# Late sums and table steps after the first trio's critical step, and Q's last stores between the loads of Q's tiles

## The reference

```
Q, K, V = x @ Wq, x @ Wk, x @ Wv              # 8 heads of 64
score   = exp(clip((K[src] * Q[dst]).sum(-1) / 8, -5, 5))   # per edge and head
wV, Z   = segment_sum(V[src] * score, dst), segment_sum(score, dst)
h       = x + wV / (Z + 1e-6)
out     = layernorm(x + batchnorm(h) * gamma + beta)        # batchnorm over nodes
```

## Time and profile before

| | us |
|---|---|
| median of 3 runs | 1886.88 |
| profiled execution, device time | 1886.89 |
| its span | 1885.0 |
| TensorE, VectorE, ScalarE, GpSimd busy | 1843.9, 1726.0, 1427.3, 1235.8 |

### The profile page before, as it was taken

How to read it: one execution, slowest core, us unless ns; L and a number is a source line. 1 busy time by engine, 2 the same in 40 slices (tenths; PEclk the granted TensorE clock), 3 DMA queues, 4 the chain that set the end, 5 groups by cost and what they waited for, 6 DMA issues and landing times.

```text
span 1885.0 us, 41041 instructions
## 1 busy us (share of the span) xinstructions
PE 1843.9 (98%) x7561; PEld 1290.4 (68%) x7672; DVE 1726.0 (92%) x2608; ACT 1427.3 (76%) x4699; POOL 1235.8 (66%) x1424
## 2 busy tenths in 40 slices
PE   8999999998999999999999999999999999999897
PEld 4444444446788887888888888888888888877333
DVE  8877776667999999999999999999999999999898
ACT  1112221126999999999999999999999999998867
POOL 1221112116888888888888888888888888875677
PEclk9999999998999999999999999999999999999999
DMA  5676667658999999999999999999999999999317
GB/s 207 221 252 223 223 222 247 235 195 316 365 364 358 354 356 357 372 357 360 349 365 373 348 354 358 368 357 357 345 368 362 361 360 353 369 360 370 118 34 290
DMA packets 191291, 589.09 MB, mean 313 GB/s; under 512 B 29104, under 2 KB 30864, under 8 KB 191248
## 3 DMA queue, kind: packets, MB, share of 16 engines
q0 software_dynamic: 135904, 465.14, 67.1%
q1 hardware_dynamic: 51888, 121.69, 17.8%
q10 hardware_dynamic: 3456, 1.78, 0.4%
HBM read 535.27 MB, written 78.91 MB: 326 GB/s over the span
## 4 chain that ended last, share of the span: by engine, by line
PE 57%; DVE 23%; issue 7%; DMA 7%; ACT 3%; POOL 2%; ACTq 1%; POOLq 0%; SPq 0%; DVEq 0%
PE places L390 21%; PE acc L1110 21%; PE q_ps L1094 12%; DVE kv L968 9%; DVE raw L979 7%; DMA kv<-kv_d,idx 5%; POOL kv L924 2%; DVE stats L1463 1%; ACT kv L1019 1%; DVE agg L1447 1%; PE mm_ps L1120 1%; DVE agg L1456 1%; DVE raw L972 1%; DMA q_tile<-xb_d 1%; DVE kv L886 1%
## 5 line engine op out<-in xcount | busy, mean ns | idle before, releaser
L924 POOL DMA_INDIRECT kv<-kv_d,idx x880 | 892.8, 1014 | 242.0 <-issue 202.9
L1019 ACT ACTIVATE kv<-kv 128x64 f32<-128x64 f32 x3520 | 889.1, 335 | 14.3
L1110 PE MATMUL acc<-kv,mm_rest 128*128 128x260 f32 x2640 | 634.6, 383 | 3.5 <-POOL kv L886 2.2
L1110 PEld LDWEIGHTS acc<-kv,mm_rest 128*128 128x128 f32 x2640 | 489.9, 189 | 105.1 <-issue 27.7
L968 DVE TENSOR_TENSOR kv<-q_ps,kv 128x1024 f32<-128x1024 f32 x440 | 536.5, 1219 | 16.5 <-DMA kv<-kv_d,idx 10.7
L979 DVE TENSOR_REDUCE raw<-kv 128x16 f32<-128x1024 f32 x440 | 533.1, 1212 | 0.0
L1094 PE MATMUL q_ps<-q_tile,mm_rest 128*128 x1320 | 422.1, 441 | 5.1 <-DVE kv L968 4.9
L390 PE MATMUL places<-w_sb,s_sb 128*128 128x512 f32 x704 | 305.9, 593 | 3.4 <-issue 3.1
L1094 PEld LDWEIGHTS q_ps<-q_tile,mm_rest 128*128 128x128 f32 x1320 | 247.6, 189 | 53.7 <-DVE kv L968 10.4
L886 DVE TENSOR_TENSOR kv<-kv 128x384 f32<-128x384 f32 (+1 forms) x440 | 272.3, 619 | 0.0
L390 PEld LDWEIGHTS places<-w_sb,s_sb 128*128 128x128 f32 x704 | 133.1, 190 | 172.9 <-issue 165.3
(11 more groups left out here) (202 smaller groups left out, 1482.8 us busy)
## 6 DMA issues: line engine op xcount, KB each, us to landing
kv_d<-kv SPq DMA_DIRECT2D x98, 256.0 KB, 2.2
q_tile<-q_d SPq DMA_DIRECT2D x49, 512.0 KB
kv<-kv_d,idx POOLq DMA_INDIRECT x880, 6.4
xb<-in_x POOLq DMA_DIRECT2D x49, 256.0 KB, 4.2
xb_d<-xb POOLq DMA_DIRECT2D x49, 256.0 KB, 6.5
out_rows<-agg SPq DMA_DIRECT2D x49, 256.0 KB, 2.1
x_sb<-in_xT SPq DMA_DIRECT2D x16, 768.0 KB, 6.5
q_d<-q_c SPq DMA_DIRECT2D x16, 512.0 KB, 2.6
```

The lines of the kernel that those rows point to most:

```text
L924: pool.indirect_dma_start(kv[:, s, u, 0:2 * DIM], None, kv_d, bass.IndirectOffsetOnAxis(idx[:, s, u:u + 1], 0), bounds_check=N_NODES - 1, ...
L1019: return act.activation(v, v, ACT.Copy, scale=kv[:, s, u, 2 * DIM + h:2 * DIM + h + 1])
L1110: last = pe.matmul(acc[:, bass.ds(par, 1), DIM - (1 - n) * HALF:DIM + n * HALF], m, kv[:, sc, u, DIM + n * HALF:DIM + (n + 1) * HALF], sta ...
```

## The change

The last x sums of trio 0 (X3, X8, X7) and T8 move from ahead of the loop to behind k_out(0) of trio 0. All numbered table steps come two slots later (`tables(3g - 2)`, `(3g - 1)`, `(3g)` for `(3g)`, `(3g + 1)`, `(3g + 2)`), ScalarE's `sign` with them, and `ends` comes just ahead of step 0. The four last Q stores leave project; in attend SyncE does two loads, a store, two loads, a store, and so on for four stores, then the loads up to tile 39, a wait for all stores, and the rest.

```diff
@@ project, sync
-                if g == TRIOS - 1:
-                    sp.wait_ge(soft["s_g0"], 32)
-                store_q(c, split_of(g, 2), q_c, s_qc)
-                store_q(a, split_of(g, 0), q_a, s_qa)
-                store_q(b, split_of(g, 1), q_b, s_qb)
-            store_q(LONE, TILES, q_d_lone, s_qc)
+                if g < TRIOS - 1:
+                    store_q(c, ...); store_q(a, ...); store_q(b, ...)
+        last_q = ((3 * TRIOS - 1, q_c, s_qc), (3 * TRIOS - 3, q_a, s_qa), (3 * TRIOS - 2, q_b, s_qb), (LONE, q_d_lone, s_qc))
@@ project, scalar
-                for b in digits_after(3 * g):          # and 3g + 1, 3g + 2
+                for b in digits_after(3 * g - 2):      # and 3g - 1, 3g
@@ project, vector
-                dve.tensor_tensor(weight(T8), weight(B11), weight(T13), ALU.add).then_inc(s_wt, 1)
             def weight_sums_last():
+                dve.tensor_tensor(weight(T8), weight(B11), weight(T13), ALU.add).then_inc(s_wt, 1)
@@ def x_sums_first(g):
+                if g == 1:
+                    dve.wait_ge(s_sums, summed(0, X7))
@@ def tables(n):
-                if n < VTILES:
+                if n == 0:
+                    dve.wait_ge(s_dl, 16)
+                    tab(dve.tensor_tensor(ends[:, :], dl[:, :], k128[:, :], ALU.add))
+                if 0 <= n < VTILES:
                     visits(n)
@@ ahead of and in the loop over trios
-            x_sums_last(0)
-            dve.wait_ge(s_dl, 16)
-            tab(dve.tensor_tensor(ends[:, :], dl[:, :], k128[:, :], ALU.add))
-                tables(3 * g)                          # slot 0
+                tables(3 * g - 2)
                 dve.wait_ge(s_dec, decoded(g, 5))
+                if g == 0:
+                    x_sums_last(0)
-                tables(3 * g + 1)                      # slot 1
+                tables(3 * g - 1)
-                tables(3 * g + 2)                      # slot 2
+                tables(3 * g)
@@ attend, sync
             sp.wait_ge(soft["s_tb"], 48)
-            sp.wait_ge(soft["s_qa"], 16 * (TILES // 3))
-            ...
-            with sp.Fori(2, TILES) as t:
+            for name in ("s_qa", "s_qb", "s_qc"):
+                sp.wait_ge(soft[name], 16 * (TILES // 3 - 1))
+            sp.wait_ge(soft["s_split"], TILES)
+            for n, (t, q, done) in enumerate(last_q):
+                with sp.Fori(2 + 2 * n, 4 + 2 * n) as u:
+                    load_in_turn(u)
+                sp.wait_ge(s_q, 16 * (4 + 2 * n))
+                sp.dma_start(q_d[t * P:(t + 1) * P, :], q[:, :, :].rearrange("p a n -> p (a n)")).then_inc(done, 16)
+            with sp.Fori(2 + 2 * len(last_q), Q_KEPT) as t:
+                load_in_turn(t)
+            (waits for all Q stores)
+            with sp.Fori(Q_KEPT, TILES) as t:
+                load_in_turn(t)
```

More of the change, by code:

```diff
@@ L54 @@
 SQ_RING = 7
+Q_KEPT = 40
 X_SLOTS = 6
@@ L315, in _ @@
                 store_k(c, k_out(2), s_kva)
-                if g == TRIOS - 1:
-                    sp.wait_ge(soft["s_g0"], 32)
-                store_q(c, split_of(g, 2), q_c, s_qc)
-                store_q(a, split_of(g, 0), q_a, s_qa)
-                store_q(b, split_of(g, 1), q_b, s_qb)
-            store_q(LONE, TILES, q_d_lone, s_qc)
+                if g < TRIOS - 1:
+                    store_q(c, split_of(g, 2), q_c, s_qc)
+                    store_q(a, split_of(g, 0), q_a, s_qa)
+                    store_q(b, split_of(g, 1), q_b, s_qb)
         @block.gpsimd
@@ L534, in _ @@
                 act.copy(held(M1), place(BANK_1)).then_inc(s_kc, 1)
-                for b in digits_after(3 * g + 1):
+                for b in digits_after(3 * g - 1):
                     sign(b)
@@ L549, in _ @@
                 high(q_b, held(U), s_qb, 16 * g)
-                for b in digits_after(3 * g + 2):
+                for b in digits_after(3 * g):
                     sign(b)
@@ L587, in weight_sums_third, with weight_sums_last @@
                 dve.tensor_tensor(weight(T6), weight(B12), weight(T0), ALU.subtract).then_inc(s_wt, 1)
+            def weight_sums_last():
                 dve.tensor_tensor(weight(T8), weight(B11), weight(T13), ALU.add).then_inc(s_wt, 1)
-            def weight_sums_last():
                 dve.wait_ge(s_wq[1], 16)
@@ L787, in _, with attend @@
                     low(q_d_lone, place(BANK_7), TILES)
-                tables(3 * g + 2)
-def attend(nc, block, kv_d, q_d, lb_d, nb_d, xb_d, tabs, agg, rz, kv, first, x_first, s_first, s_slots, soft):
+                tables(3 * g)
+        return last_q
+def attend(nc, block, kv_d, q_d, lb_d, nb_d, xb_d, tabs, last_q, agg, rz, kv, first, x_first, s_first, s_slots, soft):
     lb, nb, q_tile, zeros, less, eps, mm_first = first
@@ L892, in load, with load_in_turn @@
                              q_d[bass.ds(t * P, P), :]).then_inc(s_q, 16)
-            sp.wait_ge(soft["s_tb"], 48)
-            sp.wait_ge(soft["s_qa"], 16 * (TILES // 3))
-            sp.wait_ge(soft["s_qb"], 16 * (TILES // 3))
-            sp.wait_ge(soft["s_qc"], 16 * (TILES // 3 + 1))
-            with sp.Fori(2, TILES) as t:
+            def load_in_turn(t):
                 used = sp.value_load(cnt_row[0:1, bass.ds(t - 2, 1)], min_val=1, max_val=VISITS)
@@ L902, in _ @@
                 load(t)
+            sp.wait_ge(soft["s_tb"], 48)
+            for name in ("s_qa", "s_qb", "s_qc"):
[8 more added lines that the diff above has]
+                load_in_turn(t)
+            sp.wait_ge(soft["s_qa"], 16 * (TILES // 3))
+            sp.wait_ge(soft["s_qb"], 16 * (TILES // 3))
+            sp.wait_ge(soft["s_qc"], 16 * (TILES // 3 + 1))
+            with sp.Fori(Q_KEPT, TILES) as t:
+                load_in_turn(t)
             for t in range(FIRST_X):
@@ L1526, in program @@
         block = ctx.enter_context(nc.Block())
-        project(nc, block, xT, x, wq, wk, wv, beta, edges, dlast, xb_d, kv_d, q_d, t_d, cnt_d, lb_d, nb_d, tabs, kv, first, soft)
+        last_q = project(nc, block, xT, x, wq, wk, wv, beta, edges, dlast, xb_d, kv_d, q_d, t_d, cnt_d, lb_d, nb_d, tabs, kv, first, soft)
         agg = sb("agg", [P, TILES, AGG], F32)
@@ L1531, in program @@
         s_first, s_slots = (ctx.enter_context(nc.semaphore(name)) for name in ("s_first", "s_slots"))
-        attend(nc, block, kv_d, q_d, lb_d, nb_d, xb_d, tabs, agg, rz, kv, first, x_first, s_first, s_slots, soft)
+        attend(nc, block, kv_d, q_d, lb_d, nb_d, xb_d, tabs, last_q, agg, rz, kv, first, x_first, s_first, s_slots, soft)
         normalise(nc, block, xb_d, gamma, out, tabs, agg, rz, kv, first, x_first, s_first, s_slots, soft)
```

## The result

The changed kernel takes 1892.98 us, the median of 6 runs (1891.96 to 1897.65), against 1886.82 for the kernel before in 6 runs (1884.3 to 1889.61). The ratio is 1.0036, with a 95% interval of 1.0026 to 1.0046: the change makes the kernel 6 to 7 us slower (6.2 by the medians, 6.8 by the ratio). The forecast was 1890.7.

What follows compares the result with a forecast made beforehand. The prediction took the projection as bound by TensorE and attention by VectorE. From 1886.89 us, -3.05 + 8.6 + 2.6 - 4.8 + 0.5 = +3.85 gave 1890.7 us, range 1883 to 1896.

Steps and rivals of the forecast that it cites:

- Step 7's shift: The table step making block numbers and releasing GpSimd's table work moves to trio 3, 15.83 us later against TensorE's work.
- Rival A: Head of trio 4: row loads are in time after all, row 12 before 130 us; 1879.5 us, chance 0.10.
- the straight transfer: Trio 4: the 15.8 us delay passes undiminished to row 12, landing at 140.1, so TensorE stands 10.1 us.
- Rival C: Trio 4: short stand (5 to 6 us) or clock does not fall; 1885.5 to 1887 us, chance 0.17.
- The stand: TensorE idle before P9 of trio 4, waiting on late x rows: +8.6 us, bounds 5 and 13.
- rival D: Trio 4: the `ti` store meets the next trio's traffic, 12 us of stand; 1894.5 us, chance 0.13.
- The first hole: First trio: TensorE's wait for k_out(0) at 27.65 us goes entirely, -3.05 us, bounds 0 and -3.05.
- The clock: After the stand in trio 4, TensorE runs 5.2 us at half speed: +2.6 us, range 0 to 2.9.
- The start of attention: With Q's last four stores away, gathers land sooner and pair 4 starts earlier: -4.8 us, range -2.9 to -6.3.
- my lower bound's case: Start of attention: TensorE stays at half clock, its stretch to pair 4 only begins sooner, gaining 2.9 us.
- Q's stores in the steady part: Attention: each store right behind a load lengthens VectorE's waits for gathers, +0.5 us in all, range 0 to 5.
- Rival B: Attention's start gives nothing in the end, DMA is the bound and bytes only move; +8.15, 1895.0 us, chance 0.15.

Runs made afterwards that it cites:

- e1: The changed kernel with GpSimd's table work at its trio 4 in place of 3, first chip: 2080.95 us, 0.9981 of the kernel before.
- e5: Same kernel as e1 (GpSimd's table work one trio later than in the changed kernel), second chip: 2081.08 us, 0.9981 of the kernel before.
- e10: Same kernel as e1 (GpSimd's table work one trio later than in the changed kernel), third chip: 2080.74 us, 0.998 of the kernel before.
- e2: The kernel before with only the table steps and ScalarE's signs two slots later: 2095.65 us, 1.0054 of the kernel before.
- e6: The changed kernel with table steps one slot later than before in place of two: 2091.38 us, 1.003 of the kernel before.
- e9: The changed kernel itself, run on the chip of e10: 2091.46 us, 1.0031 of the kernel before.
- e3: The kernel before with only T8 and the first trio's late x sums moved behind k_out(0): 2084.18 us, 1.0002 of the kernel before.
- e7: The changed kernel with 160 small matmuls into a free bank ahead of P9 of trio 4: 2089.76 us, 1.002 of the kernel before.
- e4: The kernel before with only Q's last four stores moved between SyncE's loads: 2085.06 us, 1.0004 of the kernel before.
- e11: The kernel of e10 with Q's last four stores back in their old place: 2080.81 us, 0.9978 of the kernel before.

## Why the prediction came out as it did

**The sign and the place were right.** Step 7's shift (15.83 us against TensorE's work), the in-order chain behind it, the wait at the head of trio 4 and TensorE's stand before P9 are all in the trace; e1, e5 and e10 remove them, e2 makes them alone, e6 scales them. Rival A is refuted by the traces: row 12 landed at 137.1, which is 140.7 on the scale of before, where A wanted it before 130 and the straight transfer gave 140.1. Rival C's short stand and full clock are in neither trace of the changed kernel (10.99 and 9.21 us, clock 0.50 after each).

**The stand was under-sized: 8.6, measured 10.99** (9.21 in e9, 10.17 in e2). The straight transfer of the rows gave 10.1. I took 1.5 off because DMA would be quieter. The loads were in fact quicker (2.8 to 4.1 us to land; I had put 4.2 for the 5.3 of before), but the store of `ti` took 12.9 us, not 11.5, and GpSimd waited 4.88 for the stores of rows 6 to 8 to land, where it had waited 3.06 and 0.48 before. There were two corrections of opposite sign, and I made only the one that shortens. The lengthening one is what rival D named: Q's stores and the next trio's 768 KB load are issued at 116.2 to 119.1, while the `ti` store is on its way, and they take 9 and 12 us to land. That they are the cause is argued from the times; no run takes them away. D put the stand at 12; its own sum gives 1894.1, not the 1894.5 written.

**The first hole: -3.05, right.** That it needs the table steps moved too, e3 showed; the forecast had put both together and did not see it.

**The clock: +2.6, measured 2.0** to 2.8 where the stand was 11 and 9 us; e7 isolates it. The clock was 0.50 after the stand, and in e6 after one of 4.08. The Trainium skill, "TensorE: Matmul & The Clock Gate", section "Why this matters for your kernels", warns that such a gap is paid for; after these stands of 4.08 to 10.99 us the traces agree. But the clock also fell after shorter ones (below).

**The start of attention was over-sized: -4.8, measured -2.0, and -0.9 by the end of attention.** The gathers did what was forecast (pair 2 without a wait, at 452.25). The step that failed is "I expect the clock up". TensorE had no idle stretch longer than 1.62 us between 445.79 and 453.53, yet its clock fell between 452 and 453, and TensorE became what pairs 3 and 4 waited for (0.57 and 2.16 us). TensorE and the clock there:
```profile
450.94 1.20 PE L1113 MATMUL q_ps<-q_tile,mm_rest 128*128 x4 [1.62 <-DVE kv L987]
453.53 2.08 PE L1113 MATMUL q_ps<-q_tile,mm_rest 128*128 x4 [1.39 <-DVE kv L987]
455.68 3.83 PE L1129 MATMUL acc<-kv,mm_first 128*128 128x260 f32 x8
```
```profile
452.00:453.00 1.00, 0.14 (x1) 0.00 (x0) 0.89 (x2) 1.00 (x6) 0.70 (x2) 0.78 1.01 414
453.00:454.00 1.00, 0.47 (x1) 0.48 (x2) 1.00 (x4) 1.00 (x3) 0.69 (x2) 0.50 1.01 414
```
The trace of before already held the warning, which I did not read: after an idle stretch of only 1.83 us the clock was 0.50 from 439 to 442.
```profile
438.22 1.63 PE L1094 MATMUL q_ps<-q_tile,mm_first 128*128 x4 [1.83 <-DVE kv L968]
```
```profile
438.00:439.00 1.00, 0.78 (x3) 0.68 (x4) 0.96 (x2) 0.00 (x0) 0.93 (x1) 0.89 1.07 197
439.00:440.00 1.00, 1.00 (x6) 0.48 (x5) 0.42 (x1) 0.00 (x0) 0.69 (x2) 0.50 0.67 254
```
With the clock down again it was my lower bound's case (-2.9), and it came out smaller still: TensorE's stretch at half clock began 7.59 us after pair 0 where the bound had it at 7.06, and took 7.44 to pair 4 where it had 7.05. Of the 2.0, 1.2 went again by the last pair; VectorE's later waits for TensorE are 4.3 us in 5 times (463 to 1745), before 3.1 in 3 (456 to 1736). Which of these belong to the change and which to the execution, one trace of each does not tell: e1, e5 and e10, one kernel, take 1490.7, 1491.0 and 1492.2 us from pair 0 to the last pair, so that 0.9 is within what single traces differ by.

**Q's stores in the steady part: +0.5, not seen.** VectorE waited 4.3 us for gathers after the start, 4.4 before, never more than 0.7 at a time. Rival B (+8.15) has the size of the profiled execution (+8.0), and its first words, that attention's start gives nothing in the end, nearly came true (-0.9). Its reason, the DMA bound, is not what this trace shows. On the three chips e4 and e11 found the stores to be worth nothing; that is what B expects, but it does not show B's reason, since VectorE's waits there are open. No run has the stores alone in the state of the recorded result.

The sum on the profiled execution: -3.05 for the hole, -0.6 for an earlier start (0.35 of it TensorE's first product, at 13.33 for 13.68), +11.0, +1.5 and -0.9, -0.1: +7.9, against +3.85 forecast. Of the gap of 4.1 the stand is 2.4 and attention 3.4, the clock and the start take 1.7 off. That the forecast lies within 2.3 us of the median is in part luck: its two large errors, 5.8 us together, were both too hopeful, and what hid more than half of that was the 1.7 and a median run 1.85 us shorter than the profiled one.

e1's kernel beats the kernel before on all three chips, and the changed kernel on the one where both ran. It was not run where attention takes 2.95 us a pair; from the median of the changed kernel, less the stand (10.99) and the clock term (1.5) of its trace, it would come near 1893.0 - 12.5 = 1880.5 there, which is an estimate.

## What to carry to other kernels

When a step moves in a hand-written order, look for the queue of another engine that waits for it *in order*, and list what stands behind that wait. Here the readers of the tables were all in time, and the loss came from loads that have nothing to do with tables. A schedule in which a load lands just as it is needed has its slack in the trace: four adds took 2.79 us for 2.4, and that was the whole warning.

## What the runs showed of the hardware

The length of one idle stretch did not tell whether TensorE's clock falls. In dense fp32 matmuls it stayed full after one of 3.05 us and fell after one of 2.37 (e6, 0.63 at 42 to 43 us). At the start of attention it fell after one of 1.83 (before, 438 to 439), and in the changed kernel only in the third of 1.42, 1.62 and 1.39, with 1.2 to 2.1 us of matmuls between them. Nor does the kernel alone decide: in e10 the clock was 0.50 at 437 to 440, in e1 and e5, the same kernel, it was 1.00 there (the idle stretch before it was 1.75, 1.60 and 1.45). What does decide it, these runs do not show.

After stands of 4.08, 9.21 and 10.99 us the 16 records after them took 3.1, 2.8 and 2.1 us longer. With small matmuls in the stand (e7) they took no longer.

A store of 3.5 KB, issued behind seven gathers, took 10.5 to 12.9 us to land (e10 and the changed kernel; 11.9 before), longer than the 256 KB stores of x beside it (in the median 8.2 before, 4.3 in the changed kernel).

The same kernel took 1887 us in the recorded result and 2084 to 2085 on each of three chips later, with the projection unchanged and attention, for the changed kernel, at 3.39 in place of 2.95 us a pair.
